# First edge stage of a four-layer graph network: the node mask made by another engine, payload slots released by other events, block numbers loaded at another place

## The reference, cut to what matters

```python
s = s @ W_nl0;  v = einsum('nmi,mk->nki', v, W_nl1)         # node table, 160 values a node
w = relu(edge_feature @ W_fc1) @ W_fc2                      # 224 weights an edge
w0, w1, w2, w3, w4 = split(w, [64, 128, 160, 192])
xs, xv = s[dst], v[dst]                                     # gather by edge
out0a = w0 * xs
out0b = w3 * (einsum('emi,ei->em', xv, sh1) / sqrt(3))      # scalar product with the edge's direction
out1a = (w1 * xs)[:, :, None] * sh1[:, None, :]
out1b = w2[:, :, None] * xv
out1c = w4[:, :, None] * (cross(xv, sh1[:, None, :]) / sqrt(2))
agg = segment_sum(concatenate([...]), src, num_segments=N)  # 480 values an edge, summed per node
```

## Time and profile before

| | |
|---|---|
| median of 3 runs | 21244.48 us (21201.72 to 21290.81) |
| the profiled execution, its own time | 21241.17 us |
| its span in the profile | 21239.5 us |
| `edge_layer0` in it | from about 2530 us to 5832 us, 432 steps |
| busy in 2530 to 5832: PE / DVE / ACT / POOL | 1963 / 2745 / 1423 / 1947 us |
| granted TensorE clock there / after it | 0.81 / 0.98 |
| mean busy share of the DMA engines there | 0.57 |

### The profile page before, as it was taken

The page is one execution under the profiler, slowest core; times in us unless marked ns, Lnnn a source line. Parts: engine busy times, 40 slices in busy tenths (PEclk is TensorE's granted clock), DMA queues, the critical chain, the costliest instruction groups (busy, mean ns, idle before and its releaser), DMA issues. The chain is left out here.

```text
span 21239.5 us, 463275 instructions
## 1 busy us (share of the span) xinstructions
PE 17764.3 (84%) x121874; PEld 14187.1 (67%) x121874; DVE 16408.4 (77%) x45070; ACT 11695.0 (55%) x37578; POOL 12354.7 (58%) x13048
## 2 busy tenths in 40 slices
PE   2777666656569999999999999879998888999888
PEld 1333322222258888888888888779997668999766
DVE  3777788888758888888899888765555886555688
ACT  1222244444437777777777777547775225777422
POOL 2777666656537767666677676447774005777300
PEclk8887788888889999999999999999999999999999
DMA  2666555555674444444444444432223002222200
GB/s 85 172 170 171 152 112 111 110 108 111 101 238 122 123 122 123 122 122 122 122 123 123 123 122 123 129 96 67 67 67 47 6 6 51 67 67 67 34 6 6
DMA packets 1922899, 2132.27 MB, mean 100 GB/s; under 512 B 745585, under 2 KB 1597713, under 8 KB 1922545
## 3 DMA queue, kind: packets, MB, share of 16 engines
q0 software_dynamic: 567456, 1314.26, 23.5%
q1 hardware_dynamic: 1355344, 816.91, 16.1%
HBM read 1518.49 MB, written 611.44 MB: 100 GB/s over the span
## 5 line engine op out<-in xcount | busy, mean ns | idle before, releaser
L1625 POOL DMA_INDIRECT e_rows<-x,e_take x3456 | 3338.6, 966 | 1155.0 <-issue 1071.4
L1659 ACT ACTIVATE e_hot<-e_hot,e_here 128x128 f32<-128x128 f32 x10368 | 3123.2, 387 | 1403.9 <-DVE e_hot L1682 1385.5
L629 PE MATMUL e_sums<-e_feat,e_same 128*128 128x480 f32 x3456 | 1958.0, 722 | 1335.7 <-DVE e_feat L697 1335.7
L1645 PE MATMUL e_sums<-e_rows,e_hot 128*128 128x128 f32 x20736 | 2882.1, 275 | 0.0
L613 POOL DMA_INDIRECT e_rows<-table,e_take x1728 | 1932.1, 1118 | 1321.2 <-issue 1287.5
L1645 PEld LDWEIGHTS e_sums<-e_rows,e_hot 128*128 128x128 f32 x20736 | 2682.3, 192 | 0.0
L629 PEld LDWEIGHTS e_sums<-e_feat,e_same 128*128 128x128 f32 x3456 | 799.5, 244 | 2494.1 <-issue 2402.2
L1200 ACT ACTIVATE e_m<-e_th,e_yt 128x64 f32<-128x64 f32 x6480 | 2300.8, 426 | 0.0
L648 ACT ACTIVATE e_feat<-e_feat,e_pay 128x64 f32<-128x64 f32 x5184 | 1284.7, 334 | 1768.6 <-DVE e_feat L672 1735.7
L1062 POOL DMA_INDIRECT e_srow<-src_table,e_at x1620 | 1612.4, 995 | 925.9 <-issue 917.7
L1073 POOL DMA_INDIRECT comb<-e_crow,e_at x1620 | 1669.2, 1030 | 803.2 <-issue 508.0
(11 more groups left out here) (330 smaller groups left out, 46394.2 us busy)
## 6 DMA issues: line engine op xcount, KB each, us to landing
e_pay<-pay_rows SPq DMA_DIRECT2D x432, 470.0 KB, 3.9
order_keys<-key_row SPq DMA_DIRECT2D x810, 128.0 KB
e_keys<-key_row SPq DMA_DIRECT2D x810, 128.0 KB, 3.4
comb<-n_comb SPq DMA_DIRECT2D x600, 164.0 KB, 2.0
e_rows<-x,e_take POOLq DMA_INDIRECT x3456
order_feat<-in_attr_T SPq DMA_DIRECT2D x810, 64.0 KB
e_basis<-in_attr_T SPq DMA_DIRECT2D x1620, 32.0 KB
e_comps<-in_attr_T SPq DMA_DIRECT2D x1620, 32.0 KB
```

Source lines behind the costliest of these rows:

```text
L629: ins = pe.matmul(sums[b][q // G][:, 0:AGG0], same[b][:, q, :], feat[b][:, q, 0:AGG0], start=q % G == 0, stop=q % G == G - 1)
L1625: pool.indirect_dma_start(out=rows[t.j][:, q, 0:D], out_offset=None, in_=x, in_offset=bass.IndirectOffsetOnAxis(ap=take[t.j][:, q:q + 1], ...
L1645: ins = pe.matmul(bass.AP(o.tensor, o.offset, [o.ap[0], [DOT - CS * c, 2], [1, CS]]), one[:, q, 2 + c, :], bass.AP(r.tensor, r.offset, [r. ...
L1659: ins = act.activation(one[:, q, 2 + c, :], one[:, q, 0, :], ACT.Copy, scale=here[t.j][:, q, TOWARDS + c:TOWARDS + c + 1])
```

## The change

Three parts, all in `edge_layer0`:

- The mask is made by ACT. Four instructions of 128x128 write `apart = (place - column)^2` with ACT's Square (scale -1, the place as bias), placed between the copy of line 642 and the 12 scaled copies; one instruction of 128x512 writes `same = Relu(1 - apart)` behind those copies. Both counts are whole numbers, so the mask is 1 where they agree and 0 elsewhere. DVE's comparison (674) is gone. PE waits for `same_set` as well, and ACT for its own semaphores `same_set` and `apart_set`.
- SP may reload a payload slot when DVE's `feats` and ACT's `sv_set` of the group four back are counted, no longer when PE has counted its sums.
- The two block numbers of group s-4 are loaded inside `products(s-3)`: the first behind `along`, the second behind `V2`. The adds stay where they are.

```diff
+        apart = ph.sb("apart", [P, QUAD, P])
...
                         if s.reuses(RING):
                             sp.wait_ge(meta_out[s.j], s.dma(1))
-                            sp.wait_ge(sums_ps, s.count(PER * (1 - RING), PER))
+                            sp.wait_ge(feats, s.count(1 - RING))
+                            sp.wait_ge(sv_set, s.count(1 - RING))
...
                     pe.wait_ge(feats, t.count(1))
                     pe.wait_ge(sv_set, t.count(1))
+                    pe.wait_ge(same_set, t.count(1))
...
             def _(act):
+                act.wait_ge(cleared, 2)
...
                     act.activation(rows[t.j][:, :, D:EXT], rows[t.j][:, :, CS:CS + 2 * CV], ACT.Copy).then_inc(ext_set, 1)
+                    if t.reuses(1):
+                        act.wait_ge(same_set, t.count(0))
+                    for q in range(QUAD):
+                        ins = act.activation(apart[:, q, :], iota[:, :], ACT.Square, scale=-1.0, bias=pay[t.j][:, q, LO:LO + 1])
+                    ins.then_inc(apart_set, 1)
                     act.wait_ge(scalars_set, t.count(1))
...
                     ins.then_inc(sv_set, 1)
+                    act.wait_ge(apart_set, t.count(1))
+                    act.activation(same[b][:, :, :], apart[:, :, :], ACT.Relu, scale=-1.0, bias=1.0).then_inc(same_set, 1)
...
+                def number(t, k):
+                    return dve.value_load(g.blk[0:1, bass.ds(t.t() * PER + k, 1)], min_val=0, max_val=BLOCKS - 1) if t.exists() else None
+
-                def products(t):
+                def products(t, p):
...
-                    dve.tensor_tensor(same[b][:, :, :], bcast(iota[:, :].unsqueeze(1), (P, QUAD, P)),
-                                      bcast(w[:, :, LO:LO + 1], (P, QUAD, P)), ALU.is_equal).then_inc(same_set, 1)
...
                     turned(along, 0, 0).then_inc(along_set, 1)
+                    first = number(p, 0)
                     dve.wait_ge(ext_set, t.count(1))
...
                                       bcast(w[:, :, 2 * CS:2 * CS + CV].unsqueeze(2), (P, QUAD, 3, CV)), ALU.mult)
+                    second = number(p, 1)
                     dve.wait_ge(along_set, t.count(1))
...
+                t, p = s.back(3), s.back(4)
+                numbers = products(t, p) if t.exists() else [number(p, k) for k in range(PER)]
...
                         for k in range(PER):
-                            number = dve.value_load(g.blk[0:1, bass.ds(t.t() * PER + k, 1)], min_val=0, max_val=BLOCKS - 1)
-                            at = acc[:, bass.ds(number * AGG0, AGG0)]
+                            at = acc[:, bass.ds(numbers[k] * AGG0, AGG0)]
```

More of the change, by code:

```diff
@@ L567, in edge_layer0 @@
         pay_in, meta_out = ph.sems_of("pay_in", RING), ph.sems_of("meta_out", RING)
-        (consts, cleared, take_set, ext_set, same_set, scalars_set, along_set, sides_set, dots_set, cross_set, feats, sv_set, sums_ps,
-         added) = (ph.sem(n) for n in (
+        (consts, cleared, take_set, ext_set, same_set, scalars_set, along_set, sides_set, dots_set, cross_set, feats, sv_set, apart_set,
+         sums_ps, added) = (ph.sem(n) for n in (
              "consts", "cleared", "take_set", "ext_set", "same_set", "scalars_set", "along_set", "sides_set", "dots_set", "cross_set",
-             "feats", "sv_set", "sums_ps", "added"))
+             "feats", "sv_set", "apart_set", "sums_ps", "added"))
         SV, CR, DOT, S0, V2, T1 = 0, 192, 288, 320, 384, AGG0
@@ L595, in step @@
                         sp.dma_start(meta_of[:, bass.ds(t.t() * QUAD, QUAD), :], pay[t.j][:, :, LO:LO + META]).then_inc(meta_out[t.j], 16)
-                run_steps(sp, step, 1, RING, STEPS, [(PER * RING, PER * (j + 1 - RING)) for j in range(RING)] + [(16, 16 * c) for c in (-1, 0, 1)])
+                run_steps(sp, step, 1, RING, STEPS, [(RING, c) for c in range(1 - RING, 1)] + [(16, 16 * c) for c in (-1, 0, 1)])
                 for k in range(RING):
@@ L698, in products @@
                                       bcast(w[:, :, 2 * CS + 2 * CV:WNUM].unsqueeze(2), (P, QUAD, 3, CV)), ALU.mult).then_inc(feats, 1)
+                    return first, second
                 def step(s):
@@ L703, in step @@
                         indices(t)
[L704 to L707, removed]
+                    t, p = s.back(3), s.back(4)
+                    numbers = products(t, p) if t.exists() else [number(p, k) for k in range(PER)]
+                    t = p
                     if t.exists():
                         for k in range(PER):
-                            number = dve.value_load(g.blk[0:1, bass.ds(t.t() * PER + k, 1)], min_val=0, max_val=BLOCKS - 1)
-                            at = acc[:, bass.ds(number * AGG0, AGG0)]
+                            at = acc[:, bass.ds(numbers[k] * AGG0, AGG0)]
                             dve.wait_ge(sums_ps, t.count(k + 1, PER))
```

## The result

The changed kernel takes 20569.79 us (median of 4 runs, 20552.77 to 20586.14); the kernel before 21250.26 us in the runs beside them. The ratio is 0.968, interval 0.9662 to 0.9699. The gain is 680 us, where 474 were forecast; the time lies 80 us under the range. The profiled execution has a span of 20572.0 us, 667.5 less than before.

The account below looks back on a forecast made before the run. DVE's own stream plus a sometimes late payload was taken as the bound: 7.44 - 0.61 - 0.45 - 0.12 + 0.42 - 0.44 = 6.24 us a step. Over 412 steps, less 20 us for late data, this gave 20765 us, range 20650 to 20950.

Parts of the forecast that it names:

- The bound and the step count: Message stage: 7.44 us a step from DVE's own stream plus a sometimes late payload; some 412 of 432 steps alike.
- The comparison: DVE's mask comparison in each step: removing it saves 0.61 us, bounds 0.60 and 0.66.
- the loads out of the adds: Before DVE's two adds: moving the block-number loads away saves 0.45 us at the first and 0.12 at the second.
- The loads arrive between products: Behind `along` and `V2`: each moved load delays the next DVE product by 0.21 us, +0.42 a step, bounds 0 and +1.16.
- rival 3: Loads among DVE's products hide wholly: gain 1.62 us a step, 20575 us, chance 0.07; their opposite, 21050 us, 0.03.
- The payload wait, -0.44: DVE's wait before `take`: freeing the payload slot earlier removes it, 0.44 us a step, or 0.22 if only half hidden.
- What must hide: Other engines' work beside a 6.24 us step: ACT 5.2 us, POOL 5.67, PE 6.22 when slow, DMA share 0.67.
- the rows' slack of 2.9 us: POOL's gathered rows: the last lands 9.6 us after a `T1` and is wanted at 12.5, two steps on.
- the signs of a wrong prediction: In the changed profile: table loads every step, PE awaiting Relu, POOL without pauses, DVE awaiting `rows`, load at a product's end.
- Rival 1: POOL's gathers, if all take 1.32 us, set a step of 6.48 us: gain 0.96, time 20845 us; chance 0.12.
- Rival 2: Payload or rows stay late as a DMA share of 0.67 stretches transfers: gain 0.76 a step, 20930 us; chance 0.08.
- Rival 4: ACT changes tables for Square, two loads a step: 7.9 us a step, slower at 21440 us; chance 0.04.

## Why the prediction was wrong

By its steps:

- *The bound and the step count: right.* 7.44 us of DVE stream plus payload wait; some 412 steps gained, the last ones nothing.
- *The comparison, -0.61, and the loads out of the adds, -0.45 and -0.12: right.* The timeline shows 0, 0.47 and 0.21 at those places.
- *"The loads arrive between products", +0.42: the step that failed.* I read from the load's first start (4911.1) on the last product's start (4911.13) that a load can't begin before the product in front of it. The two fell together for another reason: that product waits for the subtraction before it, which ends at 4911.0, and this wait held the sequencer (4910.46 + 0.54):

  ```profile
  4910.46 0.54 DVE L693 TENSOR_TENSOR e_left<-e_left,e_right 128x384 f32<-128x384 f32 x1
  ```

  Without such a wait it is 0.7 to 1.2 us ahead, and less in one step of four (0.3 in the one read above). The cost was 0. 0.42 x 412 = 173 us, most of the 206 us by which the gain was missed. This was rival 3, with a chance of 0.07 and a time of 20575; I gave it too little, since one step's rows, with one wait in front of the load, can't tell the two readings apart.
- *The payload wait, -0.44: right in kind, a little small.* From the second add to `take` a step lost 0.51 us, since a wait also costs the 0.08 us by which instructions otherwise overlap. Start to start, on the mean from 3000 to 4900 us, the terms close: 7.47 - 0.62 (comparison) - 0.45 (first add) - 0.10 (second add, with 0.02 of new waits for sums) - 0.51 (`take`) + 0.02 (`T1`, with 0.05 of new waits for rows and sums) = 5.81 us, the step that was measured. The 0.05 taken off for late data was near. That rival 3's 20575 lies only 5 us from the result is in part luck: the larger payload term and the new waits nearly cancel.
- *What must hide: hidden, but partly not as written.* ACT's four Squares took 1.26 us together (386 ns each, overlapping) and the Relu 614 ns, near the 1.2 and 0.6 of the estimate. The mask was to come before the last product in every step; PE waited for it in 100 of 327. ACT waited 0.69 us a step for gathered rows, and the prediction had counted the rows' slack of 2.9 us against `T1` alone. ACT's copy of the same rows wants them earlier, by the prediction's own order at 6.24 + 4.1 = 10.3 us, 0.7 after they land (9.6), and at the step that was measured at 9.9. PE took most of the delay, and DVE lost 7.6 us in 327 steps to late sums. PE waiting for the Relu and DVE waiting for rows stood among the signs of a wrong prediction; both came, too small to move the time.
- *Rival 1 (POOL):* its gathers stayed at 1.12 us, and the run without `S0` shows that it doesn't bind. The Trainium skill's rule in "GPSIMD Engine Reference", section Specifications, that VectorE instructions with two SBUF inputs contend with GpSimd, would fit the 1054 ns with one such product less. But the comparison was such an instruction too, and without it the gathers were not shorter (1153 ns in the run with the mask alone, 1118 in the kernel before), so these runs neither show the rule nor rule it out. *Rival 2:* the DMA share rose to 0.72, as 0.56 x 7.47/5.81 gives for the shorter step; the payload was in time, and the rows were late for ACT but hardly for DVE. *Rival 4:* four Squares and a Relu in each step, and still two table loads in the whole trace; this agrees with the filler rule of "ScalarE: Activation LUTs" in the Trainium skill, section Table sets: the hidden batching unit. That Square needs no table of its own beside Copy and Relu is what this trace shows; that section doesn't list it.
- *The range* took in half-hidden loads and not wholly hidden ones, though the item on the loads had "nothing" as its lower bound.

## What to carry to other kernels

Put register loads and address arithmetic where the engine has instructions queued and none of them has just waited for a result of its neighbour; there they are free, while right behind such a wait most of their time is paid (0.92 of 1.4 us here). Free a buffer by its last readers, not by the consumer of what they made: here that was worth 230 us alone and 450 with a shorter stream, because a late input takes back what is saved elsewhere. When several parts change a pipeline, price each with the others in place as well as alone.

## What the runs showed of the hardware

- DVE's sequencer ran up to 1.2 us ahead of its engine. A register load of 0.31 us with 0.27 us of register work was wholly hidden by that. The lead was smaller in one step of four, and there a load showed first when `S0` was gone (0.24 us).
- A wait of DVE costs more than its idle time: 0.08 us of overlap with the instruction in front is lost, and `T1` started 0.19 us after a `take` that had waited, 0.13 after one that hadn't.
- Gathers in which all descriptors read one row of HBM slowed a step from 5.5 to 9 us, at a DMA share of 0.89 and 91 GB/s; 128 different rows removed it.
- TensorE's granted clock between 3000 and 4900 us rose from 0.81 to 0.90 with the same products, as the pauses between groups shrank (PE's busy share went from 0.61 to 0.70). The prediction had the direction, not a size. DVE waited for PE's sums 7.6 us in that stretch, so the time has next to nothing from it.
